# Small VectorE chains woven between large operations, two row scalings moved from ScalarE to VectorE, and a shorter reciprocal root in a four-layer GNN kernel

## The reference

```python
h = maximum(layernorm(x), 0);  x = x + L0(h)   # two GAT layers (with self loops), elu between them
h = maximum(layernorm(x), 0);  x = x + L1(h)   # graph attention: q, k, v = h@Wq, h@Wk, h@Wv
h = maximum(layernorm(x), 0);  x = x + L2(h)   # h@W.T+b to unit length, times 1.5*sigmoid; softmax over edges; tanh(|u|) u/|u|
h = maximum(layernorm(x), 0);  x = x + L3(h)   # two GCN layers and a last product
```

## Time and profile before

| what | value |
|---|---|
| median of three runs | 5989.83 us (5942.16, 5989.83, 5991.57) |
| profiled execution, first to last instruction | 5993.1 us |
| VectorE, TensorE busy | 77%, 77% of the span |
| POOL, ScalarE busy | 58%, 49% |
| dense stage | about 84 to 1860 us |
| GAT one, GAT two | to about 2640, 3420 us |
| EdgePass, third SoftPass | to about 4430, 4950 us |
| TurnedPass one, two | to about 5390, 5993 us |

### The profile page before, as it was taken

One profiled execution on the slowest core, in us unless ns is written; L12 is line 12 of the kernel. 1 busy time (PEld: TensorE's weight loads), 2 busy tenths in 40 slices (PEclk: granted clock), 3 DMA queues, 4 the chain that ended last, 5 costly groups with the idle time before them and its releaser, 6 DMA issues. The chain is left out here.

```text
span 5993.1 us, 77451 instructions
## 1 busy us (share of the span) xinstructions
PE 4608.6 (77%) x21160; PEld 3351.9 (56%) x21160; DVE 4603.5 (77%) x13478; ACT 2965.7 (49%) x7524; POOL 3500.3 (58%) x3009
## 2 busy tenths in 40 slices
PE   3888888888884888865777778888857674887887
PEld 3666666666663666643565545555534443665555
DVE  5888888888886888847999647777768887985554
ACT  2777777777772444432444435555545552331111
POOL 3555445454524767728888278777725433546777
PEclk9999999999996999987888889999978887998998
DMA  3666666667663444425777535555536774554444
GB/s 119 239 242 247 237 243 241 244 242 244 240 236 128 125 123 129 128 71 174 256 243 250 200 110 155 147 151 155 154 103 217 249 241 151 169 159 132 140 156 130
DMA packets 651621, 1096.83 MB, mean 183 GB/s; under 512 B 88390, under 2 KB 471814, under 8 KB 651069
## 3 DMA queue, kind: packets, MB, share of 16 engines
q1 hardware_dynamic: 525754, 837.10, 41.0%
q0 software_dynamic: 125440, 254.79, 14.7%
HBM read 523.88 MB, written 575.95 MB: 184 GB/s over the span
## 5 line engine op out<-in xcount | busy, mean ns | idle before, releaser
L830 PE MATMUL mm<-w,tt 128*128 128x264 f32 x3136 | 736.9, 389 | 0.8 <-ACT tt L874 0.8
L830 PEld LDWEIGHTS mm<-w,tt 128*128 128x128 f32 x3136 | 585.5, 192 | 92.5 <-ACT tt L874 1.0
L1318 POOL DMA_INDIRECT aim<-F,index x392 | 551.7, 1407 | 119.5 <-issue 119.2
L768 POOL DMA_INDIRECT xd<-in_x_dram,index x196 | 218.4, 1114 | 676.0 <-DMA XD<-xd 645.1
L1318 POOL DMA_INDIRECT got<-F,index x392 | 491.9, 1255 | 204.7 <-issue 111.2
L1476 ACT ACTIVATE rows<-acc 128x260 f32<-128x260 f32 (+1 forms) x588 | 227.4, 387 | 623.4 <-PE acc L1467 623.4
L796 POOL DMA_INDIRECT place<-PLACE,place_ix x392 | 425.2, 1085 | 119.5 <-issue 119.5
L820 PE MATMUL tp<-ident,h 128*128 128x128 f32 x1568 | 236.8, 284 | 323.9 <-ACT h L914 162.0
L1463 PE MATMUL acc<-got,sel 128*128 128x260 f32 (+1 forms) x1176 | 425.8, 449 | 74.8 <-DVE sel L1438 68.2
L2487 DVE SCALAR_TENSOR_TENSOR agg<-mask,agg,acc 128x128 f32<-128x128 f32 x784 | 251.8, 343 | 253.5 <-PE acc L2474 144.2
L830 PE MATMUL mm<-wl,tt 128*128 128x264 f32 x1568 | 419.4, 389 | 6.0 <-ACT tt L874 5.8
(11 more groups left out here) (348 smaller groups left out, 13645.7 us busy)
## 6 DMA issues: line engine op xcount, KB each, us to landing
F<-f1o SPq DMA_DIRECT2D x97, 528.0 KB
F<-f2o SPq DMA_DIRECT2D x97, 528.0 KB, 3.4
HL<-ho SPq DMA_DIRECT2D x97, 528.0 KB, 3.7
xin<-in_x_dram SPq DMA_DIRECT2D x97, 512.0 KB
H<-h SPq DMA_DIRECT2D x97, 512.0 KB, 3.7
X<-x3o SPq DMA_DIRECT2D x97, 512.0 KB
out_dram<-oo SPq DMA_DIRECT2D x97, 512.0 KB
drow<-DSTF SPq DMA_DIRECT2D x84, 448.0 KB
```

Of the source, the lines that this page charges most:

```text
L768: nc.gpsimd.indirect_dma_start(out=xd[:, n % 2, t, :], out_offset=None, in_=x, in_offset=bass.IndirectOffsetOnAxis(ap=index[:, tile, 1:2], ...
L830: last = nc.tensor.matmul(mm[PAIR[stage, q]][:, r, 0:F2W], lhs[:, q, 2 * r + k, :], w[:, k, :], start=(k == 0), stop=(k == KB - 1))
L1318: nc.gpsimd.indirect_dma_start(out=buf[:, n % SLOTS, t, :], out_offset=None, in_=table, in_offset=bass.IndirectOffsetOnAxis(ap=index[:, n ...
```

## The change

- **Chains.** `restart` and its drains are gone from all stages. A chain's semaphore counts on through a stage. Where the drain had also kept a buffer from being overwritten too early, a wait on an existing semaphore stands now (`diff`, in the SoftPasses).
- **Root.** `rsqrt` has seven operations in place of eleven.
- **Dense stage, VectorE.** `statistics` runs one iteration later and is cut into steps that stand one by one between large operations, beside the steps of `scales` (now for unit n-6), `gate` and `norms` (now for unit n-5). `oo`, `g` and `x1` are done in halves. One half of `f1o` moves to the start of the next iteration. Rows 2 and 3 of the four `ho` scalings are done here (semaphore `ho2`).
- **Dense stage, ScalarE.** h1 rows of unit n+1 (`first_rows`) come last in iteration n, tanh stands just before `ho`, `ho` has two rows, and elu's steps and the halves of `hr` alternate.
- **Buffers and queues.** `xin` has six slots in place of four and is loaded four units ahead; `hr` has three. SP issues HL's store first and X3's an iteration later; TensorE waits for g by halves. The arithmetic of the dense stage's products is as before.

```diff
+    n = link.go(V.tensor_scalar(y.bitcast(I32), v.bitcast(I32), -0.5, RSQRT_SEED, ALU.mult, ALU.add))
...
-    for f in (1.0, 1.0, times):
...
-        n = link.go(V.scalar_tensor_tensor(y, a, 1.5 * f, y, ALU.add, ALU.mult))
...
+    for c in (c2, c1):
         link.need(n)
-        n = link.go(V.tensor_tensor(a, y, y, ALU.mult))
+        n = link.go(V.scalar_tensor_tensor(a, a, c, h, ALU.add, ALU.mult))
+    n = link.go(V.scalar_tensor_tensor(y, a, c0, y, ALU.add, ALU.mult))
...
-                            hold(pe, s["g"], b.n + 1, pp)
                             for q in range(2):
+                                hold(pe, s["g"], b.n * 2 + (q + 1), pp)
                                 turn_half(g, q, turns_before(at, "b"))
...
+                    def first_rows(n):
+
+                        if 0 <= n < U:
+                            hold(act, s["stats"], n + 1, pa)
+                            if n:
+                                hold(act, s["tp_h"], turns_before(At(n - 1, 0, 0, 4), "c"), pa)
...
-                        if a.alive(U):
-                            hold(act, s["stats"], at.n + 1, pa)
...
-                        if d.alive(U):
...
                         if z.alive(U):
                             hold(act, s["f1_h"], z.n * 2 + 2, pa)
...
-                        if e.alive(U):
-                            hold(act, s["unc"], e.n + 1, pa)
-                            nc.scalar.activation(th[:, :], unc[:, :], ACT.Tanh).then_inc(s["tanh"], 1)
+                        if d.alive(U):
+                            hold(act, s["x3"], d.n - 2, pa)
+                            hold(act, s["ho"], d.n - 2, pa)
+                            hold(act, s["ho2"], d.n - 2, pa)
+                            third_product(d, 0)
                         if z.alive(U):
                             hold(act, s["zm"], z.n + 1, pa)
...
+                        if d.alive(U):
+                            third_product(d, 1)
+                        if a.alive(U):
+                            copy_turned(at, "a", a, 0)
                         if c.alive(U):
-                            hold(act, s["stats"], at.n + 1, pa)
+                            hold(act, s["stats"], at.n + 2, pa)
...
+                            hold(act, s["unc"], e.n + 1, pa)
+                            nc.scalar.activation(th[:, :], unc[:, :], ACT.Tanh).then_inc(s["tanh"], 1)
                             hold(act, hl_out[e.slot], 16 * e.use, pa)
-                            for r in range(G):
-                                last = nc.scalar.activation(ho[:, e.slot, r, 0:258], hr[:, e.slot, r, 0:258], ACT.Copy,
+                            for r in range(2):
+                                last = nc.scalar.activation(ho[:, e.slot, r, 0:258], hr[:, e.n % 3, r, 0:258], ACT.Copy,
...
+                        first_rows(at.n + 1)
+                    first_rows(0)
...
+                    def statistics(n):
...
+                        link.need(max(moments.values()))
+                        hold(dve, s["stats"], n + 1, pv)
+                            hold(dve, s["sq"], n - 4, pv)
+                            link.go(V.tensor_scalar(var[:, 2 * G:3 * G], n2[:, (n - 5) % 2, :], 1e-24, None, ALU.max))
+                        hold(dve, s["h1_h"], min(n, U) * 2, pv)
+                        hold(dve, s["h2"], min(n - 4, U), pv)
+                        yield from rsqrt(nc, link, rt[:, n % 2, :], var[:, :], ra[:, :], ROOT)
+                        V.scalar_tensor_tensor(nm[:, n % 2, :], mean[:, :], -0.5, rt[:, n % 2, 0:2 * G],
+                                               ALU.mult, ALU.mult).then_inc(s["stats"], 1)
...
+                    def gate(d):
+                        hold(dve, s["sq"], d + 1, pv)
...
+                        k = link.go(V.tensor_scalar(fac[:, d % 2, :], em[:, d % 2, :], 1.0, None, ALU.add))
+                        yield
+                        link.need(k)
+                        k = link.go(V.reciprocal(fac[:, d % 2, :], fac[:, d % 2, :]))
...
                     def scales(e):
...
+                        hold(dve, s["tanh"], e + 1, pv)
+                        V.tensor_tensor(ga[:, :], th[:, :], per[:, :], ALU.mult)
+                        k = link.go(V.tensor_scalar(gb[:, :], th[:, :], 1e-8, None, ALU.add))
...
+                    def unit(n):
+                        a, z, b, d, e, f = n, n - 1, n - 2, n - 4, n - 5, n - 6
+                        steps = statistics(n)
+                        ends = scales(f) if alive(f) else iter(())
+                        gates = gate(e) if alive(e) else iter(())
+                        sizes = norms(n, e) if alive(e) else iter(())
+                        take(steps, 1)
+                        if alive(z):
+                            evacuate(z, "a", "mma_h", f1o[:, z % 2, :, 0:F2W], rb1, "f1_h", 1)
+                        take(steps, 1)
+                        take(ends, 1)
+                        for r in range(G):
+                            if alive(n + 2):
+                                row_stats(n + 2, r)
+                            take(steps, 1)
+                            take(ends, 1)
+                        take(ends)
+                        if alive(f):
...
+                        for r in range(G):
+                            if alive(f):
+                                last = V.scalar_tensor_tensor(x3o[:, f % 2, r, :], hr[:, f % 3, r, 0:D], ga[:, r:r + 1],
+                                                              x1[:, f % 4, r, :], ALU.mult, ALU.add)
+                            take(steps, 1)
+                            take(gates, 1)
+                        if alive(f):
+                            last.then_inc(s["x3"], 1)
+                        take(steps, 1)
+                        if alive(f):
+                            hold(dve, s["x3"], f + 1, pv)
...
+                        for q in range(2):
...
+                            if alive(f):
+                                V.tensor_tensor(oo[:, f % 2, half, :], x3o[:, f % 2, half, :], wide(gcn_const, D, 2),
+                                                ALU.add).then_inc(s["oo"], 1)
+                            take(steps)
+                            if q == 0 and alive(d):
+                                hold(dve, s["hr_h"], d * 2 + 2, pv)
+                                V.tensor_scalar(em[:, d % 2, :], hr[:, d % 3, :, 258], -87.0, None, ALU.max)\
+                                    .then_inc(s["em"], 1)
+                            take(sizes, 1)
+                        for q in range(2):
...
+                            if alive(z):
+                                hold(dve, s["exp"], z + 1, pv)
+                                hold(dve, s["tp_h"], turns_before(At(n, 0, 0, 4), "a"), pv)
+                                V.scalar_tensor_tensor(g[:, half, :], zm[:, half, :], -1.0, f1o[:, z % 2, half, 0:D],
+                                                       ALU.add, ALU.max).then_inc(s["g"], 1)
+                            take(sizes, 1)
+                        if alive(b):
...
+                            for q in range(2):
+                                evacuate(b, "b", "mmb_h", f2o[:, b % 2, :, :], rb2, "f2_h", q)
+                                take(sizes, 1)
+                            hold(dve, s["h2"], b - 3, pv)
+                            for q in range(2):
...
+                                hold(dve, s["f2_h"], b * 2 + (q + 1), pv)
+                                V.tensor_tensor(x1[:, b % 4, half, :], xin[:, b % XS, half, :], f2o[:, b % 2, half, 0:D],
+                                                ALU.add).then_inc(s["x1"], 1)
+                                hold(dve, s["x1"], b * 2 + (r // 2 + 1), pv)
+                                moments["x1"] = link.go(V.bn_stats(st[:, G + r, :], x1[:, b % 4, r, :]))
+                        take(sizes)
+                        if alive(e):
...
+                            for r in range(2, G):
+                                last = V.tensor_scalar(ho[:, e % 2, r, 0:258], hr[:, e % 3, r, 0:258], fac[:, e % 2, r:r + 1],
+                                                       None, ALU.mult)
+                            last.then_inc(s["ho2"], 1)
+                        if alive(a):
...
+                            evacuate(a, "a", "mma_h", f1o[:, a % 2, :, 0:F2W], rb1, "f1_h", 0)
+
+                    for r in range(G):
+                        row_stats(0, r)
+                    for n in range(-1, U + 6):
+                        unit(n)
...
+                hold(dve, self.done["diff"], n, None)
...
-                        link.restart()
```

(47 more changed lines are left out.)

216 lines of the change are left out of this document (92 added, 124 removed).

## The result

The changed kernel takes 5580.7 us (median of 4 runs, 5569.6 to 5583.5) against 5990.7 us (4 runs, 5942.2 to 5994.4): a ratio of 0.931, 95% interval 0.928 to 0.935. It is 410 us faster; 344 were forecast, and the time lies 9 us under the range. The profiled execution is the shortest of its runs, 5569.6 us, so the two traces differ by 425.3 us, 15 more than the medians.

A forecast was written before the change was run, and what follows sets the result against it. A loop through several engines was taken to bound the dense stage, and TensorE after the change. 92 iterations at 3.5 us give 322, plus 20 and 2 elsewhere: 344 off 5993.1, rounded to 5650 us, range 5590 to 5770.

The forecast's parts named there:

- The loop: Dense stage: the loop nm, h1, tanh, gb, nm sets the old pace, 17.62 us a unit; the change opens it.
- TensorE's own work, 13.9: Dense stage: TensorE's turnings and multiplies, untouched by the change, sum to 13.9 us a unit.
- 0.2 for handovers: Dense stage: added to TensorE's 13.9 us for handovers that don't quite close, making 14.1 us a unit.
- The 12 iterations of filling and emptying I take at nothing.: Dense stage's ends: lost drains and part of a root, 16 us, against an added set of moments; taken as no gain.
- VectorE, 13.6: Dense stage: VectorE's own work a unit, with woven small operations at 0.08 us each, sums to 13.6 us.
- rival two: Dense stage: weaving hides nothing, VectorE becomes the bound at 16.5 us a unit, 5870 us in all; chance 0.05.
- ScalarE and h2: Dense stage: ScalarE falls to 12.6 us a unit; h2 is the tightest handover, with 0.75 us to spare.
- Rival one: Dense stage: TensorE still waits for h2, 14.9 to 15.8 us a unit, 5720 to 5805 us; chance 0.20.
- Rival three: Dense stage: transfers become the bound and the kernel slower, 19.0 us a unit, 6100 us; chance 0.03.
- The first TurnedPass: Stage after the dense one: a drain and four small operations fewer a group; 20 us gained, between 0 and 59.
- The two signs: First TurnedPass, would show the forecast wrong: mask starts under 7.5 us apart, or ScalarE's h waits for TensorE in most groups.
- Other edge stages: GATs, EdgePass: shorter root only lengthens VectorE's waits; third SoftPass and GAT one gain 2 us from drains, bounds 0 and 43.

The follow-up runs named there:

- edge_and_dense_root: The kernel before with the change's stages behind the dense one, and the seven-operation root in its old dense stage, drains and order kept: 5889.5 us, 16.91 a unit.
- only_opened: The change, but its dense stage keeps only the new stage order: chains in one piece, 11-operation root, two drains, four ho rows on ScalarE: 5820.5 us.
- half_of_c: The change without the four products adding c's bias, and with only the first half of product c's depth added up: 5501.1 us, 13.05 a unit.
- chains_in_blocks: The change, but VectorE issues each chain of small operations in one piece instead of step by step between large operations: 5755.9 us, 15.69 a unit.
- squares_first: The change, but ScalarE makes the four squares and em's exponential before h2, not behind it: 5675.0 us, 14.87 a unit.
- the eleven traces: The change and ten of the twelve follow-up runs, all with the short root behind the dense stage: first lg to end 4063.7 to 4080.2 us, mean 4072.
- old_root: The change, but with the 11-operation root everywhere, woven as the short one is: 5609.8 us, 13.78 a unit.
- edge_only: The change, but with the dense stage, its root and its drains of the kernel before: 5978.7 us, ratio 0.995 to 1.000 to the kernel before.
- drains_back: The change with two VectorE drains put back into each dense-stage iteration, one at its start and one before oo: 5576.2 us, 13.78 a unit.

## Why the prediction was right in kind and too small

*The loop.* Right. The chain from `nm` over h1 and tanh to `gb` set the pace: four operations fewer in it moved the unit by 0.82 us (edge_and_dense_root), and with it opened both waits of the earlier trace rows are gone.

*TensorE's own work, 13.9, and 0.2 for handovers.* The sum is 13.77. I had priced the turnings at 0.93, from one that began after an idle time; without a wait it is 0.87 or 0.88. The 0.2 for handovers that "don't quite close" was not needed: with 0.71 us to spare at the tightest place and VectorE's 13.05 under it, all of them close. Both together are 0.33 us a unit. On the two traces the 92 intervals gave 352.0 us, 30.0 more than 322.

*"The 12 iterations of filling and emptying I take at nothing."* This step failed, by 34.6 us, 2.9 an iteration. With them in the sum the range would have begun at 5555 and held the time. Five of the 97 intervals between two `em` lie in these iterations: the first two took 38.2 us and take 27.8, the last three 39.3 and 31.6, together 18.2 less. 12.8 more came before the first `em` and 3.6 behind the last. A filling iteration runs through the same loop as a full one as soon as `nm`, h1 and the first product are alive: the old kernel's second interval, 17.81 us, already has the full pace. The root alone shortened the time to the first `em` by 3.9 us (edge_and_dense_root), opening the loop by 10.5 (only_opened, 140.5 to 130.0). I had the gain of those iterations only as lost drains and part of a root, 16 us, and cancelled it.

30.0 and 34.6 are the 64.6 us by which the dense stage's 322 fell short of 386.6.

*The range.* Its lower end was also added up wrongly. By the prediction's own terms, 13.9 us a unit and 80 us elsewhere, it is 5993.1 - 92 x 3.72 - 80 = 5571, not 5590, and would have held the time. That would have been luck: a unit takes less than 13.9, and the iterations at the ends were still at nothing.

*VectorE, 13.6.* Measured 13.05 (half_of_c). The steps were right (0.08 woven, 0.20 behind a dependent step), the large operations a little cheaper than summed. It stayed off the path, as forecast. By the rule of the Trainium skill (page "VectorE: DVE Perf Modes", section "Rules for kernel authors") the woven order and chains_in_blocks, with the same operations, should take the same time. They differ by 1.92 us a unit: rival two's mechanism is refuted, and its price, 16.5, lies 0.8 above what VectorE's blocks cost (15.69).

*ScalarE and h2.* ScalarE measured 0.917 x 13.77 = 12.6 as forecast; h2 had 0.71 to spare (0.75 forecast), and when I used it up the price came out as computed (squares_first). Rival one's place was real; its wait did not occur.

*Transfers.* 87% busy at 13.77, forecast 87% at 14.1, without holding anything; even 93% did not (half_of_c). Rival three is out.

*The first TurnedPass.* 20 forecast, 20.5 on the traces; the size was right and the wait behind it misread. `mask` and ScalarE's h answer to the earlier trace rows:

```profile
L2528 DVE TENSOR_TENSOR mask<-drow,dst_before x30: 683/686/692, 4683.8 to 4898.0; 128x512 f32<-128x512 f32 x30
```

```profile
4704.83 2.07 ACT L2674 ACTIVATE h<-got,nm,rt 128x256 f32<-128x256 f32 x4 [4.27 <-PE acc L2540]
```

A group takes (4898.0 - 4683.8) / 29 = 7.39 us, 0.45 less than 7.84. The row of h in the earlier trace rows was not the usual case. These are the waits of h before (5080 to 5300 us):

```profile
ACT h L2609 <- DVE nm L2549: 104.2, 22, 5.6
ACT h L2609 <- PE acc L2474: 30.2, 6, 5.9
```

And after (4680 to 4900 us):

```profile
ACT h L2674 <- PE acc L2540: 125.8, 29, 6.2
```

Before, h waited for VectorE's `nm` in 22 of 28 groups; now it waits for TensorE's accumulation in all but one. So VectorE's chain, with the root in it, was what h waited for in most groups, and it gained until TensorE's accumulation came last. That the middle of the bounds met 20.5 is luck as far as the reason goes. The two signs that I had named against the forecast (under 7.5 us, and that wait in most groups) both appear: the first could not tell 20 us from something else, since 20 / 49 makes 7.43 us a group, and the second shows the change of the wait.

*Other edge stages.* 2 forecast, within 0 to 43; 18 on the two traces, most of it the third SoftPass (11.3), and about 11 by the mean of the eleven traces (31 less 20). I had let a shorter root there only lengthen VectorE's waits and had priced the drains. old_root shows the reverse: the root counts, and taking the drains out brought nothing that can be seen. This term was mis-sized by 9 to 16 us.

## What to carry to other kernels

When a loop through several engines sets a pace, write down each engine's own work first: the fullest one is the pace after opening, and most of the gain a unit falls on the iterations that fill and empty the pipeline too. A small operation costs the time until the next one can start, not the time that it lasts; put other work between dependent ones before counting them out or moving large ones away. Time by edit here, taken in this order: opening 1.25 us a unit, root, drains and moved rows 0.70, weaving 1.92. Another order would share it out differently, and weaving in the old loop was not tried. And read who waits for whom from a count over many groups: one row in order of time can be the rare case.

## What the runs showed of the hardware

- A VectorE operation on 4 to 12 elements a partition starts 0.07 to 0.09 us behind an independent one and 0.19 to 0.21 behind the one that it needs, though most last 0.15 to 0.17 in both cases. Most of the difference counts as busy time: chains_in_blocks took 15.69 us a unit and half_of_c, with the same operations on VectorE, 13.05, and 1.9 of these 2.6 us read as busy (95% against 99.7%).
- Which operation a wait names matters: with the count one operation later, the step behind it came 0.1 us later, and a unit of the old loop took 0.09 us more (edge_only against before).
- A drain between woven operations took 0.18 to 0.19 us of VectorE (drains_back), and nothing of the kernel's time while VectorE had it to spare.
- TensorE's turning of 8 blocks takes 0.93 us start to start if it begins after a wait and 0.87 without one (both in squares_first: 904.64 to 905.57, 914.04 to 914.91).
- At 310 to 327 GB/s and 87 to 93% busy DMA engines the dense stage's transfers still delayed nothing on its path.
